# A graph network's edge stage: messages in a PSUM bank of their own, and the sums of three steps back at the start of PE's step

## What is computed

```python
xn = (x - mean) * rsqrt(var + eps) * gamma + beta        # batch norm over the nodes
feat = concatenate([xn[dst], xn[src] - xn[dst]], axis=-1)
h = relu(feat @ W1 + b1)                                  # 128 -> 128
msg = h @ W2 + b2                                         # 128 -> 64
agg = segment_max(msg, dst, num_segments=N)               # 0 where a node has no edge
out = layernorm(x + relu(agg), axis=-1)
```

## Time and profile before

| what | value |
|---|---|
| median of 3 runs | 2415.8 us (2410.23 to 2418.83) |
| profiled execution | 2424.7 us; span 2422.7 us |
| mean granted TensorE clock | 0.878 of full speed |
| PE busy | 1818.5 us, 75% of the span |
| DVE, POOL, ACT busy | 1292.7, 1283.2, 862.0 us (53%, 53%, 36%) |
| DMA | 202.31 MB, mean 84 GB/s |

### The profile page before, as it was taken

How to read it: one execution, slowest core, us unless ns; L and a number is a source line. 1 busy time by engine, 2 the same in 40 slices (tenths; PEclk the granted TensorE clock), 3 DMA queues, 4 the chain that set the end, 5 groups by cost and what they waited for, 6 DMA issues and landing times.

```text
span 2422.7 us, 31826 instructions
## 1 busy us (share of the span) xinstructions
PE 1818.5 (75%) x12305; PEld 938.5 (39%) x12305; DVE 1292.7 (53%) x2070; ACT 862.0 (36%) x968; POOL 1283.2 (53%) x1356
## 2 busy tenths in 40 slices
PE   2046887787878778787878878878788778887785
PEld 1032444343434434343434444444444434444443
DVE  2054655565555555555555556556456555565553
ACT  2044443333333333333333333333334333333333
POOL 7715245556555565456555565555655565555621
PEclk6557899998999999898989899998999988898996
DMA  4154223233333332333323333233323333333320
GB/s 93 35 173 122 59 84 81 77 90 86 80 86 84 88 95 70 85 81 96 87 70 91 87 87 80 81 89 95 89 72 94 91 81 81 75 94 87 76 62 5
DMA packets 132832, 202.31 MB, mean 84 GB/s; under 512 B 74828, under 2 KB 76937, under 8 KB 132648
## 3 DMA queue, kind: packets, MB, share of 16 engines
q0 software_dynamic: 43440, 85.03, 16.5%
q1 hardware_dynamic: 87946, 115.04, 14.9%
q10 hardware_dynamic: 1294, 0.20, 0.1%
HBM read 189.19 MB, written 12.60 MB: 83 GB/s over the span
## 4 chain that ended last, share of the span: by engine, by line
another core or an unknown queue 38%; PE 29%; ACT 19%; issue 8%; DVE 5%; DMA 1%; SPq 0%; POOLq 0%; DVEq 0%; ACTq 0%
PE ps_g L1146 10%; PE ps_g L1153 6%; ACT hid L688 5%; ACT best L640 5%; PE ps_mr L1190 4%; ACT best L644 4%; ACT best L683 3%; PE ps_acc L1234 2%; DVE oh L919 2%; PE ps_h L1205 2%; PE ps_mr L1196 2%; PE ps_h L1215 1%; DVE runmax L993 1%; PE ps_h L1222 1%
## 5 line engine op out<-in xcount | busy, mean ns | idle before, releaser
L511 POOL DMA_INDIRECT xb<-b_dram,src_ix x1248 | 1181.1, 946 | 1031.4 <-PE ps_h L1205 384.9
L919 DVE TENSOR_SCALAR oh<-ps_k 128x1024 bf16<-128x1024 bf16 x1372 | 849.6, 678 | 1.0
L1146 PE MATMUL ps_g<-oh,xtab 128*128 128x512 bf16 x2744 | 643.5, 387 | 5.8 <-issue 5.0
L1190 PE MATMUL ps_mr<-hid,w 128*64 128x512 f32 x784 | 270.8, 776 | 369.9 <-ACT best L683 325.6
L972 DVE TENSOR_TENSOR best<-ps_acc,last_key 128x336 f32<-128x336 f32 x196 | 99.3, 507 | 815.8 <-remote 655.9
L683 ACT ACTIVATE best<-ps_mr 128x512 f32<-128x512 f32 x196 | 117.0, 597 | 1097.1 <-remote 816.3
L1146 PEld LDWEIGHTS ps_g<-oh,xtab 128*128 128x128 bf16 x2744 | 256.9, 99 | 375.6 <-issue 103.3
L1153 PE MATMUL ps_g<-oh,xtab 128*64 128x512 bf16 x2744 | 387.1, 424 | 12.6 <-issue 11.3
L993 DVE TENSOR_TENSOR_SCAN runmax<-rb,runmax,ps_mr 128x512 f32<-128x512 bf16 x196 | 249.6, 1274 | 97.4 <-PE ps_mr L1190 55.1
L688 ACT ACTIVATE hid<-ps_h,bias 128x1024 f32<-128x1024 f32 x196 | 217.9, 1112 | 106.8 <-remote 42.2
L1190 PEld LDWEIGHTS ps_mr<-hid,w 128*64 128x64 f32 x784 | 44.1, 154 | 479.6 <-ACT best L683 391.8
(11 more groups left out here) (181 smaller groups left out, 537.2 us busy)
## 6 DMA issues: line engine op xcount, KB each, us to landing
kb<-keys_dram SPq DMA_DIRECT2D x98, 504.0 KB
rb<-reset_dram SPq DMA_DIRECT2D x98, 256.0 KB
xb<-b_dram,src_ix POOLq DMA_INDIRECT x1248
src_t<-in_src SPq DMA_DIRECT2D x56, 256.0 KB
aw<-a_dram SPq DMA_DIRECT2D x196, 31.5 KB
a_dram<-oh SPq DMA_DIRECT2D x6, 672.0 KB, 3.5
xwin<-xp_dram SPq DMA_DIRECT2D x196, 10.5 KB
out<-y SPq DMA_DIRECT2D x182, 10.5 KB
```

The source lines that it names most:

```text
L511: pool.indirect_dma_start(xb[:, u, t, h, :], None, b_dram[:, :], bass.IndirectOffsetOnAxis(ap=src_ix[:, b, q + t, h:h + 1], axis=0))\
L919: dve.tensor_scalar(oh[0:PN, n % NOH, :], node_keys_ps, n % TN + 0.5, None, ALU.is_equal).then_inc(oh_ready, 1)
L1146: last = pe.matmul(ps_g[:, h, :], xtab[0:PN, t, 0:2, :].rearrange("p w c -> p (w c)"), oh[0:PN, n % NOH, h * GE:(h + 1) * GE], start=t == ...
L1190: last = pe.matmul(ps_mr[h * C:(h + 1) * C, :], w2[:, :], hid[:, j % 2, h, :], start=True, stop=True)
```

## The change

From APART = 12 (the last of the first 12 gathered steps) on, messages go to the bank ps_x, and so no longer wait for take_rows. The sums of step k-3 are issued at the start of PE's step k, ahead of turn(k-2), and the wait for rows_sb stands there (for take_rows(k-3)). sums_of(k-2) behind messages(k-1) is gone for these steps. Up to step 12, and behind step 193, the order is the old one, but that in the last steps messages(NI-2) stands ahead of its wait. DVE's scan is put into a function and reads the bank that its messages were written to.

```diff
@@ -91,6 +91,13 @@
     taken = [k for k in range(NI) if not wide_rows(k)]
 
 
+    APART = gathered[NX - 1]
+
+    def apart(k):
+        return APART <= k < LAST
+    assert 3 <= APART < picked[0] + LAST and all(wide_rows(k) or k in picked for k in range(APART + 1, NI))
+
+
     def sides(k):
         return 1 if k == 0 else 2
 
@@ -295,6 +302,9 @@
         g_hid_ps, g_hid_sb, g_msg_ps, g_msg = sem("g_hid_ps"), sem("g_hid_sb"), sem("g_msg_ps"), sem("g_msg")
         g_col, g_merged, g_block, g_acc_ps, g_acc_sb = sem("g_col"), sem("g_merged"), sem("g_block"), sem("g_acc_ps"), sem("g_acc_sb")
         g_step, g_sq, g_std, g_x_in, g_y, g_out = sem("g_step"), sem("g_sq"), sem("g_std"), sem("g_x_in"), sem("g_y"), sem("g_out")
+
+        def msg_bank(j):
+            return ps_mr if j < APART - 1 else ps_x
 
         block = ctx.enter_context(nc.Block())
 
@@ -955,6 +965,15 @@
                                       norm[:, 4, c0:c1].rearrange("p (w a) -> p w a", a=1).to_broadcast([ROWS, wn, C]),
                                       ALU.mult).then_inc(y_ready, 1)
 
+                def scan(j):
+                    w, i = divmod(j, WI)
+                    s = w % NS
+                    dve.wait_ge(msg_ps, j + 1)
+                    if i == 0:
+                        dve.wait_ge(rst_in[s], 16 * (w // NS + 1))
+                    dve.tensor_tensor_scan(runmax[:, j % 2, :], rb[:, s, i * GE:(i + 1) * GE], msg_bank(j)[:, :],
+                                           runmax[:, (j + 1) % 2, GE - 1:GE], ALU.add, ALU.max).then_inc(run_ready, 1)
+
                 n = 0
                 for k in range(NI + 3):
                     upto = ahead[min(k, NI)]
@@ -985,13 +1004,7 @@
                         node_onehot(n)
                     n = early
                     if 1 <= k <= NI:
-                        w, i = divmod(k - 1, WI)
-                        s = w % NS
-                        dve.wait_ge(msg_ps, k)
-                        if i == 0:
-                            dve.wait_ge(rst_in[s], 16 * (w // NS + 1))
-                        dve.tensor_tensor_scan(runmax[:, (k - 1) % 2, :], rb[:, s, i * GE:(i + 1) * GE], ps_mr[:, :],
-                                               runmax[:, k % 2, GE - 1:GE], ALU.add, ALU.max).then_inc(run_ready, 1)
+                        scan(k - 1)
                     for g in range(2 * k, min(2 * k + 2, XG)):
                         x_rest_piece(g)
                     for g in range(max(0, 2 * k - 2), min(2 * k, XG)):
@@ -1187,7 +1200,7 @@
 
                 def messages(j):
                     for h in range(2):
-                        last = pe.matmul(ps_mr[h * C:(h + 1) * C, :], w2[:, :], hid[:, j % 2, h, :], start=True, stop=True)
+                        last = pe.matmul(msg_bank(j)[h * C:(h + 1) * C, :], w2[:, :], hid[:, j % 2, h, :], start=True, stop=True)
                     last.then_inc(msg_ps, 1)
 
                 def turn(j):
@@ -1246,16 +1259,20 @@
                         hidden_src(k)
 
                 def older(k):
-                    if k >= 2:
+                    if k >= 2 and k < APART:
                         pe.wait_ge(rows_sb, k - 1)
                     messages(k - 1)
                     if k >= 2:
+                        pe.wait_ge(rows_sb, k - 1)
                         sums_of(k - 2)
 
                 n = 0
                 for k in range(NI - 1):
                     if 1 <= k <= 2:
                         last_piece(2 * k - 1, *LAST_GROUPS[2 * k - 1])
+                    if APART < k <= LAST:
+                        pe.wait_ge(rows_sb, k - 2)
+                        sums_of(k - 3)
                     if k >= 2:
                         turn(k - 2)
                     if k == 0:
@@ -1272,16 +1289,18 @@
                     hidden_layer(k)
                     if k <= 1:
                         last_piece(2 * k, *LAST_GROUPS[2 * k])
-                    if 1 <= k < LAST:
+                    if 1 <= k < APART:
                         older(k)
+                    if apart(k):
+                        messages(k - 1)
                     if k + 1 in picked:
                         pe.wait_ge(x_sb, taken.index(k + 1) + 1)
                     select(n, n + fill[k])
                     n += fill[k]
                 turn(NI - 3)
                 pe.wait_ge(hid_sb, NI - 1)
+                messages(NI - 2)
                 pe.wait_ge(rows_sb, NI - 2)
-                messages(NI - 2)
                 sums_of(NI - 3)
                 turn(NI - 2)
                 pe.wait_ge(rows_sb, NI - 1)
```

## The result

The changed kernel takes 2431.0 us (median of 12 runs, 2420.1 to 2439.5), the kernel before 2420.4 us (12 runs, 2410.2 to 2428.5): ratio 1.0042, 95% interval 1.0022 to 1.0062, 10 us slower. The profiled execution took 2425.6 us with a span of 2423.7, 5 us under its median, that of before was 4 us over its own, so the two traces differ by 1 us only.

The account below looks back on a forecast made before the run. POOL's gather burst was taken to clock wide steps: 9.69 + 1.81 + 0.33 = 11.83 us, without PE's work. Terms 0 + 11 - 5 + 5 + 4 = +15 on 2415.8 gave 2431, stated as 2430 us; range 2385 to 2465.

Parts of the forecast that it names:

- clocked wide steps: The 148 steps timed by POOL's gather burst: dropping the 0.65 us wait for take_rows gains 0 there.
- 40 wide steps with 8 or 9 tiles: Wide steps clear of picked ones: moved sums leave too many matmuls behind the hold, 0.27 us each, +11 us.
- one crawl: Step 75 before the change: PE's last matmuls went one at a time, 12.06 us burst to burst against 11.83.
- The sign that I named for it: Single records of rows_wide ending steps with 8 and 9 tiles, these some 0.27 us longer than those of 7.
- Costs and gains cancel: Rival: PE's run-ahead bears 48 matmuls, so no new step crawls; -5 + 4, 2415 us, chance 0.25.
- The messages start with the release: In wide steps, messages would start at the release, no longer 0.65 us behind it.
- the count of 22 matmuls done and 40 left: In a 7-tile step of 62 matmuls, 22 have started when completions are held; 40 left is the edge.
- Picked steps: Steps with POOL idle: 8 regain the 0.65 us wait, -5 us; 20 with 9-tile selects pay 0.27 us, +5 us.
- Early turns: Behind selects of 2 to 5 tiles, 1.5 more turns pass within a burst, each losing 2.9 us: +4 us.
- their turn now comes up to 0.65 us earlier: In the 16 steps with 2 to 5 tiles, this tips none to four more turns into passing mid-burst.
- The far rival: The burst's clocking yields, so 0.65 us is won in 148 to 181 steps: 2298 to 2320 us, chance 0.10.
- A finite run-ahead: Past held completions PE ran on some 34 matmuls, then one at a time; 39 or 40 left is the edge.

Follow-up runs that it names:

- Experiment 7: Changed kernel with sums behind messages, and 1 or 4 of a set's 49 tiles in the picked step, 8 or 9 in each other: 2313.6 us, ratio 0.9496.
- experiment 1: Kernel before with only the sums moved as in the change; messages stay in ps_mr and wait for take_rows: 2446.1 us, ratio 1.0023.
- experiment 2: Kernel before with only the bank changed: messages go to ps_x without waiting, sums stay ahead of select: 2416.2 us, ratio 0.9913.
- 3: Changed kernel with the sums of three steps back behind messages, except at a block's end: 2407.5 us, ratio 0.9877 to the kernel before.
- experiment 5: Changed kernel with the 49 tiles of a set spread evenly over its 6 or 7 steps: 2408.6 us, ratio 0.9870 to the kernel before.
- experiment 9: Changed kernel with four of the eight gather DMAs of each wide step left out, on chips without the hold: 1750.1 us, ratio 1.0207.
- 6: Changed kernel with the sums behind messages and each set's tiles spread evenly over its steps: 2379.3 us, ratio 0.9757 to the kernel before.
- experiment 11: Kernel before with 1 or 4 tiles in the picked step, on chips without the hold: 1724.3 us, ratio 1.0054.
- experiment 8: Kernel before with four of the eight gather DMAs of each wide step left out, on chips without the hold: 1712.9 us, ratio 0.9984.

## Why the prediction came true, point by point

The forecast was 2430 us, +15 on 2415.8; measured were 2431.0, and +10 in the ratio. The direction was right, and so was the claim that the clocked wide steps stand. But the sum came out by luck in part: a term of +11 was nothing, and a term of +4 was some +19, and the two errors cancel; some 5 us of the agreement of the absolute times come from the kernel before, whose median over 12 runs is 2420.4 and not 2415.8.

- *The clocked wide steps don't shorten* (0 us). Right: 11.82 and 11.75 us, bursts 11.83 and 11.79 apart, L693 waking 1.76 us behind the last DMA. Experiment 7 supports it from the other side.
- *40 wide steps with 8 or 9 tiles pay 0.27 us each* (+11 us). Wrong in size, it is nothing: steps behind 8 tiles went from 12.07 to 11.90 us (23), behind 9 from 12.60 to 12.60 (8), behind 7 from 11.82 to 11.80 (68). I had carried the price of one crawl over to all. The sign that I named for it failed as well: in the 71 clear wide steps, idle stretches of over 0.2 us ahead of a rows_wide matmul fell from 23 to 2; they now stand ahead of the selects, 111 against none. "Costs and gains cancel" was right on this term.
- *The messages start with the release.* Wrong, and the count of 22 matmuls done and 40 left rests on it: in the earlier trace rows's place after the change they start at 1048.07, 3.3 us ahead of the release of 1051.39. They need only the hid of the step before, and with the wait I had taken away what stopped PE in front of them.
- *Picked steps: -5 for the wait, +5 for sums in front of hidden_src.* The net of 0 was near: -3 us over the sixteen steps without an early turn. How it splits I don't know. The sums did not hold up hidden_src in these, since all four of its matmuls had started at the release. Where PE's stop is left in and only the sums move (experiment 1), 2.00 had, against 3.19 and 3.62 with the sums elsewhere (2, 3).
- *Early turns* (+4 us: one or two more, at 2.9 us). More of them did come, and with them the largest part of the loss. Mis-sized was how many: seven more at 2.0 us each, +14 us, and +5 in the three that were early before, nearly all of it in one. The step that failed is "their turn now comes up to 0.65 us earlier". In the one laid out above it came 3.42 - 1.75 = 1.67 us earlier, since I took away the wait of 0.65 us and kept PE's stop at the release. The wait had been that stop; without it PE does messages and a short select ahead of the release. The price, too, is not the early turn's alone: with the sums in their old place the two new ones of experiment 2 lost nothing.
- *Not foreseen:* PE, running ahead, comes to one-hots that don't exist yet, sits idle, and step T+1 is worked at the lower clock in 14 of 26 cases (5 before). Nine of the 14 are steps without an early turn, where it takes back most of what the others gain. That the idle time makes the clock fall is read from the windows of experiment 5 and not shown; the run that should show it could not.
- *The far rival, -96 to -118 us,* did not happen. The bank alone was worth 0.9% (experiment 2), 21 us, about a fifth of that price; with the sums moved as well the gain was gone (1.0042). The Trainium skill's page "Perfetto Trace Analysis" (Optimizing Tensor Performance, Matmuls) says that independent matmul groups should rotate through PSUM banks; experiment 2 agrees, by 0.9%.
- *A finite run-ahead.* It is seen in the changed kernel too, in the sums of 992.96 that come one at a time, as the transposes in the earlier trace rows; but in the wide steps no cost of it shows. The Trainium skill's page "TensorE: Matmul & The Clock Gate" (Architectural detail: the array is 16× 32×32, not 1× 128×128) has 64 entries for it; no run here counts them.

Open: what holds the completions, and why two chips do without; how much of the changed kernel's loss is the clock alone; whether an early turn without the moved sums is as cheap on the chip of the profiles as in experiment 2; the rest of 0.29 us a step in experiment 9.

## What to carry to other kernels

A wait that stands for 325 us among the costliest groups can be worth nothing, and it can also be what keeps an engine in step: before it is taken out, look what the engine does with the time, to the next thing that it needs. To price an event, compare each step with itself before and after, not the steps that have the event with those that don't: here the second way made 4.3 us of 2.0. Where a transfer burst clocks a step, put work into it and take work out of the steps between bursts; here that was 2.7% (experiment 7 against 6), and the change of bank 0.9%. Work moved to where it "costs nothing" should be placed by what stands behind it in the queue at the moment of release, and such a result should be measured on more than one chip before it is relied on.

## What the runs showed of the hardware

- On some chips a finished group of PE's matmuls was passed on 4.56 us late while POOL issued a burst of indirect DMAs, and on others 0.03 us behind its end (experiment 11); the same kernel takes 2420 to 2438 us on the first and 1714 to 1716 on the second.
- Around 3.69 us of idle time TensorE's granted clock went from 1.00 of full over four microseconds to 0.51 over the next four (experiment 5), and 13 matmuls of 128x512 took 5.03 us, against 3.20 for 14 at the full clock.
- From the start of 16 small float32 matmuls to the start of the next work it was 0.46 us where bf16 selects followed (experiment 8) and 0.59 us where float32 transposes did (experiment 9).
